# Residual parts of five tiles moved from VectorE to ScalarE and GpSimd, and the first tiles of the K/V loop reordered

## The chip, the cores and the metric

The kernel runs on one core of one Trainium2 chip. The metric is the device time of one execution in microseconds (us). The engines are called by their short names: PE (TensorE), DVE (VectorE), ACT (ScalarE), POOL (GpSimd) and SP (SyncE, which here issues DMAs).

## What is computed

One transformer-like block on x of 2 x 1024 tokens with 512 features, all in float32. Six modulation vectors (sa, ca, ga, sb, cb, gb) per batch come from `silu(c) @ wmod`. Cut to what matters:

```python
h = layernorm(x) * (1 + ca) + sa
Xn = layernorm(h) * gamma + beta
Q, K, V = split(Xn @ W_in + b_in)
K, V = rotary(K), rotary(V)                       # the first 256 of 512 features are turned
A = 0.5 * sum_tokens(K/|K| * V/|V|) + 0.5          # one row of 512 per batch
x2 = x + ga * ((A * Q) @ W_out + b_out + h)
h2 = layernorm(x2) * (1 + cb) + sb
out = x2 + gb * (shared_expert(h2) + top-2 of 8 routed experts(h2))
```

## The kernel before

The 2048 tokens are 16 tiles of 128 tokens (`t`, NT = 16; NB = 8 tiles per batch). Every matrix product of full accuracy is done as three products of a high and a low part (`product3`, lines 1819 to 1821: hi*hi, hi*lo, lo*hi), so each operand needs a high part, written by ACT with a rounding copy, and a low part, which DVE forms as the difference (`weights_hi`/`weights_lo`, `tokens_hi`/`tokens_lo`). Every engine has its own instruction stream, written by hand in program order; semaphores join them, and an instruction that waits holds up all that stands behind it on its engine.

**The K/V loop (about 20 to 152 us).** For each tile: DVE `x_statistics(t)` takes mean and variance of x (lines 1121 to 1123), POOL `first_power(t)` raises the variance to the power -1/2 (L593), DVE `modulated(t)` forms h (L1137, L1140) and its statistics (L1157 to L1160), POOL `second_power(t)` makes the second normalisation's factors (L598, L599), ACT `normed(t)` applies them (L735), PE `transposes(t)` turns the tile (L1867), ACT `tokens_hi` and DVE `tokens_lo` split it (L743, L1164), PE `kv_matmul(t, 0)` and `kv_matmul(t, 1)` form K and V. ACT `k_row` copies K out of PSUM, DVE `products(t)` multiplies V and K (L1189, L1190) and turns the product with the rotary tables `cs` (L1202), ACT `k_square` and `v_square` take the norms, POOL `token_weight` makes the weight of each token, and PE `weighted_sums(t)` adds the tile into A (L1949). Bank use is double buffered by t % 2.

Between these PE carries small one-off products, the list `MISC`: the rotary tables `sin_a`, `cos_a` (tiles 0 to 3) and `sin_b`, `cos_b` (tiles 4 to 7), the rows `s1`, `c1` of batch 1, the four transposes `q0` to `q3` of W_in's Q part, and others. `SLOT_A[t]` stand between K and V of tile t, `SLOT_B[t]` behind V of tile t; all but `cos_a` use one bank, so each waits until the one before it in the list was read. ACT or DVE (`BY_VECTOR`) read them one iteration later.

**The second row loop (about 169 to 280 us).** For each tile: PE `y_matmul(t)` (A-scaled Q and W_out folded into one matrix `mw`), DVE `second_rows(t)` adds the residual part `u_of(t)` (L1355) and takes statistics, POOL `third_power(t)` (L610), DVE `ffn_rows(t)` makes h2 (L1367, L1369), PE `transposes2`, ACT `tokens2_hi` (L879, L880), DVE `tokens2_lo` (L1374). The residual part, `(1 + ca) * ga` plus a column, times the normalised x of the ring `xring`, is one DVE instruction (`residual_part`, L1343) one tile ahead; ACT `x_normed` (L867) fills the ring. `shared_in_lo(t)` (t < 4, L1106) and, at t = 6, `m_block_late` and `m_block_lo_late` (L1307, L1312) also stand on DVE; the shared expert's first chunks come into PE's stream behind tiles 6, 7, 10 and 13 (`Y_CHUNKS`), and chunk 1 waits for DVE's `s_mul_of(0, 0)` (L1382) of chunk 0. `y_matmul(t)` waits for `second_rows(t - 2)`; chunk 0 of the shared expert waits for `tokens2_lo(3)`.

Behind that stand the rest of the shared expert and the routed experts, which the diff does not touch.

## Time and profile before

| | us |
|---|---|
| median of 3 runs (lowest, highest) | 663.05 (662.36, 664.44) |
| the profiled execution: its time, its span | 664.68, 662.9 |
| busy: PE, DVE, ACT, POOL | 641.3, 495.2, 268.6, 164.7 |

The profile is one execution, followed by engine. A row of a timeline gives the start in us from the span's start, the duration in us, the engine, the source line, the operation with its tiles (written tile first), the shapes and a count, and in brackets how long the engine was idle before it and what released it. Durations of neighbouring DVE and ACT rows overlap by some hundredths, so lengths of steps are best taken from start to start. A row of the waits says who waited for whom, the total, the number of times and the longest.

### The profile page before, as it was taken

To read this page: it belongs to the slowest core of one execution; us is meant where nothing else is said; L and a number is where in the kernel's file an instruction comes from. 1 tells how busy PE (TensorE), PEld (TensorE's weight loads), DVE (VectorE), ACT (ScalarE), POOL (GpSimd) and SP (SyncE) were. 2 spreads that over 40 slices of the span, in tenths; PEclk is the share of its full clock that TensorE was granted. 3 is DMA by queue.
4 is the path that set the end of the run, shared out by engine and by line. 5 is a ranking of instruction groups with operands and counts; after the bars stand their busy time and mean duration, and the time that the engine had idled before them with its cause. 6 is when DMAs were issued, how large, how long until landed. Compare 5 with 4: busy or idle time off the path is not lost.

```text
span 662.9 us, 10578 instructions
## 1 busy us (share of the span) xinstructions
PE 641.3 (97%) x3666; PEld 531.6 (80%) x3666; DVE 495.2 (75%) x1087; ACT 268.6 (41%) x525; POOL 164.7 (25%) x211
## 2 busy tenths in 40 slices
PE   7899999999998999999999999999999999999995
PEld 3577677777876788788888888899989899899994
DVE  3987779848899788637895685569769697886953
ACT  2555354443544333511202302435537455474531
POOL 1233233320011111100000002313554445453123
PEclk9999999999999899999999999999999999999998
DMA  8913031106234262513042043446877668676145
GB/s 327 386 67 112 25 105 33 32 17 207 79 112 142 80 215 96 175 46 114 0 118 97 1 143 95 135 137 205 163 147 200 95 194 153 157 184 108 47 63 63
DMA packets 41151, 80.80 MB, mean 122 GB/s; under 512 B 5019, under 2 KB 13229, under 8 KB 40566
## 3 DMA queue, kind: packets, MB, share of 16 engines
q1 hardware_dynamic: 33382, 62.06, 28.3%
q0 software_dynamic: 7728, 18.22, 15.0%
q8 instruction: 23, 0.38, 0.2%
q14 instruction: 18, 0.15, 0.1%
HBM read 58.88 MB, written 22.56 MB: 123 GB/s over the span
## 4 chain that ended last, share of the span: by engine, by line
PE 83%; DVE 11%; issue 2%; ACT 1%; DMA 1%; POOL 1%; SPq 0%; POOLq 0%; DVEq 0%
PE bank L1819 22%; PE bank L1821 22%; PE bank L1820 22%; PE bank L2131 5%; PE bank L2106 2%; PE bank L1949 1%; PE bank L2136 1%; PE bank L1885 1%; DMA xring<-in_L_attn_X 1%; PE bank L1867 1%; PE bank L2194 1%; PE bank L2086 1%; DVE st L1121 1%; POOL out_rows L679 1%; DVE hx L1367 1%
## 5 line engine op out<-in xcount | busy, mean ns | idle before, releaser
L1819 PE MATMUL bank<-xt,sgu 128*128 128x512 f32 x176 | 70.0, 398 | 5.2 <-DVE ewst L1382 2.0
L1819 PE MATMUL bank<-ht,ew 128*128 128x256 f32 (+1 forms) x256 | 74.3, 290 | 0.0
L1820 PE MATMUL bank<-ht,ew 128*128 128x256 f32 (+1 forms) x256 | 73.1, 285 | 0.0
L1821 PE MATMUL bank<-ht,ew 128*128 128x256 f32 (+1 forms) x256 | 73.0, 285 | 0.0
L679 POOL DMA_INDIRECT out_rows<-y,si x35 | 54.8, 1565 | 73.5 <-DVE y L1748 64.0
L1821 PE MATMUL bank<-xt,sgu 128*128 128x512 f32 x176 | 69.4, 394 | 0.0
L1820 PE MATMUL bank<-xt,sgu 128*128 128x512 f32 x176 | 69.2, 393 | 0.0
L1819 PE MATMUL bank<-wkv,xt 128*128 128x512 f32 x128 | 53.8, 421 | 1.4 <-DVE xt L1164 1.4
L1820 PE MATMUL bank<-wkv,xt 128*128 128x512 f32 x128 | 50.5, 395 | 0.0
L1821 PE MATMUL bank<-wkv,xt 128*128 128x512 f32 x128 | 50.5, 394 | 0.0
L1820 PEld LDWEIGHTS bank<-ht,ew 128*128 128x128 f32 x256 | 48.2, 188 | 0.0
L1819 PEld LDWEIGHTS bank<-ht,ew 128*128 128x128 f32 x256 | 48.2, 188 | 0.0
L1821 PEld LDWEIGHTS bank<-ht,ew 128*128 128x128 f32 x256 | 48.2, 188 | 0.0
L659 POOL COPY gi<-gidx 128x5 int32 (+1 forms) x8 | 4.7, 584 | 168.8 <-DVEq L1657 130.6
L667 POOL DMA_INDIRECT picked<-h_d,gi x36 | 41.3, 1147 | 17.5 <-issue 8.5
L1819 PEld LDWEIGHTS bank<-xt,sgu 128*128 128x128 f32 x176 | 33.5, 190 | 12.5 <-DVE ewst L1382 2.3
L610 POOL TENSOR_TENSOR rs<-ve,nhalf 128x1 f32<-128x1 f32 x16 | 14.9, 933 | 98.5 <-DVE ve L1123 98.5
L1821 PEld LDWEIGHTS bank<-xt,sgu 128*128 128x128 f32 x176 | 33.4, 190 | 7.2
L1820 PEld LDWEIGHTS bank<-xt,sgu 128*128 128x128 f32 x176 | 33.5, 190 | 6.4
L1819 PE MATMUL bank<-ew,gtR 128*128 128x512 f32 (+1 forms) x96 | 38.4, 400 | 0.0
L1820 PE MATMUL bank<-ew,gtR 128*128 128x512 f32 (+1 forms) x96 | 37.9, 395 | 0.0
L1821 PE MATMUL bank<-ew,gtR 128*128 128x512 f32 (+1 forms) x96 | 37.8, 394 | 0.0
(377 smaller groups left out, 1632.8 us busy)
## 6 DMA issues: line engine op xcount, KB each, us to landing
xring<-in_L_attn_X SPq DMA_DIRECT2D x32, 256.0 KB, 2.7
ewst<-in_L_ffn_w_gate SPq DMA_DIRECT2D x8, 704.0 KB, 5.4
ewst<-in_L_ffn_w_up SPq DMA_DIRECT2D x8, 704.0 KB, 4.9
slots<-in_L_wmod SPq DMA_DIRECT2D x4, 1024.0 KB, 6.7
x_d<-rows SPq DMA_DIRECT2D x16, 256.0 KB, 2.0
h_d<-hx SPq DMA_DIRECT2D x16, 256.0 KB, 2.0
xrow<-x_d SPq DMA_DIRECT2D x16, 256.0 KB, 2.7
out_rows<-xrow SPq DMA_DIRECT2D x16, 256.0 KB, 2.0
```

The source lines that it names most:

```text
L610: pool.tensor_tensor(rs[:, 2, t:t + 1], ve[:, 2, t:t + 1], nhalf[:, 0:1], ALU.pow).then_inc(rs3_ready, 1)
L667: pool.indirect_dma_start(out=picked[par][:, j, :], out_offset=None, in_=h2_d, in_offset=bass.IndirectOffsetOnAxis(ap=gi[:, par, j:j + 1], ...
L679: pool.indirect_dma_start(out=out, out_offset=bass.IndirectOffsetOnAxis(ap=si[0:CR[j], par, j:j + 1], axis=0), in_=y[0:CR[j], j, :], in_of ...
L1121: link(dve.bn_stats(st6[:, :], row))
L1367: link(dve.scalar_tensor_tensor(hx_of(t), rows_of(t), mv2[:, t, 0:1], bc_cb[:, b, :], ALU.subtract, ALU.mult))
L1819: nc.tensor.matmul(dst, a[0], b[0], start=first, stop=False)
L1820: nc.tensor.matmul(dst, a[0], b[1], start=False, stop=False)
L1821: return nc.tensor.matmul(dst, a[1], b[0], start=False, stop=last)
L1867: last = nc.tensor.transpose(bank[T_BANKS[t % 2]][:, k * P:(k + 1) * P], hz[:, 2 + t % 2, k * P:(k + 1) * P], ident[:, :])
L1885: nc.tensor.matmul(to, pairs4[:, :].to_broadcast([P, P]), (bk, bv)[i][:, :], start=False, stop=True)\
L2106: last = nc.tensor.transpose(bank[RT_BANKS[(par + s) % 2]][:, i * P:(i + 1) * P], picked[par][:, j, k * P:(k + 1) * P], ident[:, :])
L2131: nc.tensor.matmul(bank[to[c % 2]][0:n, 0:width], packed[:, k, i * P:i * P + n], tok[part][:, k, :], start=k == 0 and not part, stop=k == ...
```

## The change

In words: (1) residual parts of tiles 2 to 6: ACT's new `residual_factor` writes the factor (row plus column) into `u`, and POOL multiplies it in place with the ring's x, behind `third_power` of the tile before; DVE's `residual_part` is left for the other tiles. (2) At t = 6 DVE runs `m_block_lo_late` behind `s_mul_of(0, 0)`. (3) PE computes V's bias row before K of tile 0, in the place of three filler matmuls. (4) DVE runs `modulated(1)` ahead of `weights_lo(0)`, and `tokens_lo(0)` behind its first chunk; ACT runs `normed(1)` two weight chunks earlier; `x_statistics(2)`, `modulated(2)` and the product of the tables come later. (5) The tables and most of `MISC` move one tile later; `products` is split, and tile 0's turning (`turned_products`) runs at t = 2; PE turns tile 2 behind V of tile 1 and adds tile 0 at t = 2.

```diff
-SLOT_A = {1: ["s1"], 2: ["sin_b"], 3: ["q0"], 4: ["q2"], 6: ["qrow"]}
-SLOT_B = {0: ["sin_a", "cos_a"], 1: ["c1"], 2: ["cos_b"], 3: ["q1"], 4: ["q3"], 5: ["mod"], 6: ["qbias"], 9: ["a0"]}
+SHARED_OUT = range(2, 7)
+SLOT_A = {2: ["s1"], 3: ["sin_b"], 4: ["q0"], 5: ["q2"], 6: ["qrow"], 7: ["q3"]}
+SLOT_B = {1: ["sin_a", "cos_a"], 2: ["c1"], 3: ["cos_b"], 4: ["q1"], 5: ["mod"], 6: ["qbias"], 9: ["a0"]}
...
             for t in range(NT):
                 third_power(t)
+                if t + 1 in SHARED_OUT:
+                    pool.wait_ge(xh_ready, t + 2)
+                    pool.tensor_tensor(u_of(t + 1), u_of(t + 1), xring[:, (NT + t + 1) % GT, :], ALU.mult)\
+                        .then_inc(x_read, 1)
...
-            weights_hi(1, (1, 2, 3))
+            weights_hi(1, (1,))
             normed(1)
+            weights_hi(1, (2, 3))
             bias_row_hi(1)
             tokens_hi(1)
-            act.wait_ge(sincos, 1)
-            nc.scalar.activation(sin, sin, ACT.Square).then_inc(sinsq, 1)
             for t in range(NT):
                 if t:
                     for name in SLOT_B.get(t - 1, ()):
                         if name not in BY_VECTOR:
                             read_misc(name)
+                    if t == 1:
+                        tokens_hi(2)
+                        k_row(1)
                     v_square(t - 1)
...
                 if t + 2 < NT:
                     normed(t + 2)
+                if t == 0:
+                    act.wait_ge(sincos, 1)
+                    nc.scalar.activation(sin, sin, ACT.Square).then_inc(sinsq, 1)
...
+            def residual_factor(t):
+
+                act.wait_ge(x2_ready, t - 1)
+                nc.scalar.activation(u_of(t), bc_g[:, t // NB, :], ACT.Identity, bias=std1[:, t:t + 1])\
+                    .then_inc(xh_ready, 1)
...
                 if t >= 2:
                     tokens2_hi(t - 2)
+                if t + 1 in SHARED_OUT:
+                    residual_factor(t + 1)
                 if t + 2 < NT:
                     x_normed(t + 2)
...
-            weights_lo(0)
-            x_statistics(2)
+            modulated(1)
+            weights_lo(0, (0,))
             tokens_lo(0)
-            modulated(1)
+            weights_lo(0, (1, 2, 3))
             bias_rows(0)
             weights_lo(1)
             bias_rows(1)
             tokens_lo(1)
+            x_statistics(2)
+            modulated(2)
             dve.wait_ge(table_in, 32)
             dve.tensor_tensor(cos, cos, sin, ALU.mult).then_inc(sincos, 1)
             for t in range(NT):
+                if t == 2:
+                    turned_products(0)
                 if t:
                     products(t - 1)
+                    if t > 1:
+                        turned_products(t - 1)
...
-                if t + 2 < NT:
+                if t == 1:
+                    tokens_lo(2)
+                if 0 < t < NT - 2:
                     modulated(t + 2)
-                if 1 <= t < NT - 1:
+                if 1 < t < NT - 1:
                     tokens_lo(t + 1)
...
-                if t and t + 1 < NT:
+                if t and t + 1 < NT and t + 1 not in SHARED_OUT:
                     residual_part(t + 1)
...
-                if t == NB - 2:
-                    for i in range(DC):
-                        m_block_lo_late(i)
                 if t < DC:
                     shared_in_lo(t)
                 if t in Y_CHUNKS:
                     s_mul_of(0, Y_CHUNKS[t])
+                if t == NB - 2:
+                    for i in range(DC):
+                        m_block_lo_late(i)
...
             transposes(0)
-            keep_busy(3)
+            bias_row(1)
             for t in range(NT):
                 kv_matmul(t, 0)
-                if t == 0:
-                    bias_row(1)
-                if t + 1 < NT:
+                if t + 1 < NT and t != 1:
                     transposes(t + 1)
+                if t == 2:
+                    weighted_sums(0)
                 for name in SLOT_A.get(t, ()):
                     misc(name)
                 kv_matmul(t, 1)
+                if t == 1:
+                    transposes(2)
                 for name in SLOT_B.get(t, ()):
                     misc(name)
-                if t:
+                if t >= 2:
                     weighted_sums(t - 1)
```

## Rows read from the trace of the kernel before

**Rows 1.** Waits of PE from 60 to 280 us: line, releaser, total, times, longest.

```profile
PE bank L1819 <- DVE rows L1355: 2.3, 2, 1.2
PE bank L1819 <- DVE ewst L1382: 2.0, 1, 2.0
PE bank L1819 <- DVE xt L1374: 2.0, 1, 2.0
```

**Rows 2.** Timeline of PE, 0 to 62 us.

```profile
19.06 0.66 PE L1867 MATMUL bank<-ident,hz 128*128 128x128 f32 x4 [1.01 <-ACT hz L735]
...
25.49 1.06 PE L1856 MATMUL bank<-slots,gb_col 128*32 128x512 f32 x8
...
27.45 0.66 PE L1867 MATMUL bank<-ident,hz 128*128 128x128 f32 x4
...
32.29 0.48 PE L1819 MATMUL bank<-wkv,xt 128*128 128x512 f32 x1
...
41.12 0.41 PE L1949 MATMUL bank<-prod,wtok 128*32 128x256 f32 x2
...
58.02 0.50 PE L1819 MATMUL bank<-wkv,xt 128*128 128x512 f32 x1
```

**Rows 3.** Timeline of DVE, 0 to 62 us.

```profile
17.36 2.74 DVE L1170 SCALAR_TENSOR_TENSOR wkv<-slots,gb_col,wkv 128x512 fp32r<-128x512 f32 x4
...
29.46 1.21 DVE L1276 TENSOR_TENSOR slots<-slots 128x1024 f32<-128x1024 f32 x1
...
36.83 0.75 DVE L1137 SCALAR_TENSOR_TENSOR hz<-xring,mv,bc_c 128x512 f32<-128x512 f32 x1
...
39.48 0.68 DVE L1164 TENSOR_TENSOR xt<-bank,xt 128x512 fp32r<-128x512 f32 x1
40.07 0.69 DVE L1121 BATCH_NORM_STATS2 st<-xring 128x6 f32<-128x512 f32 x1
```

**Rows 4.** Timeline of ACT, 0 to 62 us.

```profile
30.70 1.06 ACT L818 ACTIVATE slots<-slots 128x1024 f32<-128x1024 f32 x1 [1.96 <-DVE slots L1276]
...
40.49 0.81 ACT L735 ACTIVATE hz<-hz,nm,rs 128x512 f32<-128x512 f32 x1 [1.75 <-POOL nm L599]
```

**Rows 5.** Timeline of POOL, 0 to 62 us.

```profile
1.22 0.28 POOL L583 TENSOR_SCALAR_AFFINE_SELECT ident<-ident 128x128 f32<-128x128 f32 x1 [0.24 <-POOL ident L582]
1.47 0.20 POOL L585 MEMSET gw<- 128x128 f32 x1
1.61 0.12 POOL L586 MEMSET ones<- 128x32 f32 x1
...
40.26 0.19 POOL L599 TENSOR_TENSOR nm<-mv,rs 128x1 f32<-128x1 f32 x1
```

**Rows 6.** Timeline of POOL, 152 to 240 us.

```profile
174.96 0.55 POOL L610 TENSOR_TENSOR rs<-ve,nhalf 128x1 f32<-128x1 f32 x1 [20.36 <-DVE ve L1123]
...
193.74 0.99 POOL L610 TENSOR_TENSOR rs<-ve,nhalf 128x1 f32<-128x1 f32 x1 [6.29 <-DVE ve L1123]
```

**Rows 7.** Timeline of DVE, 152 to 240 us.

```profile
188.20 0.69 DVE L1374 TENSOR_TENSOR xt<-bank,xt 128x512 fp32r<-128x512 f32 x1 [1.15 <-ACT xt L880]
...
193.57 0.74 DVE L1343 SCALAR_TENSOR_TENSOR u<-bc_c,std,xring 128x512 f32<-128x512 f32 x1
...
194.84 0.74 DVE L1367 SCALAR_TENSOR_TENSOR hx<-rows,mv,bc_gb 128x512 f32<-128x512 f32 x1
...
213.72 1.29 DVE L1312 TENSOR_TENSOR mw<-xrow,mw 128x512 fp32r<-128x512 f32 x2
...
216.13 0.68 DVE L1382 TENSOR_TENSOR ewst<-ewst,bank 128x512 f32<-128x512 f32 x1
```

**Rows 8.** Timeline of ACT, 152 to 240 us.

```profile
188.05 0.82 ACT L867 ACTIVATE xring<-xring,nm,rs 128x512 f32<-128x512 f32 x1
```

**Rows 9.** Stretches of 2 us: busy time of each engine, then PE's granted clock (full is 1.00).

```profile
218.00:220.00 2.00, 2.00 (x7) 1.53 (x6) 1.93 (x6) 0.00 (x0) 0.99 (x1) 0.50 0.36 131
220.00:222.00 2.00, 2.00 (x8) 1.61 (x7) 1.88 (x3) 0.00 (x0) 0.00 (x0) 0.65 0.41 131
```

More of the change, by code:

```diff
@@ L64 @@
 M_BLOCKS = 2 * DC - 1
+SHARED_OUT = range(2, 7)
 Y_CHUNKS = {6: 0, 7: 1, 10: 2, 13: 3}
-MISC = ["sin_a", "cos_a", "s1", "c1", "sin_b", "cos_b", "q0", "q1", "q2", "q3", "mod", "qrow", "qbias", "a0", "a1"]
+MISC = ["sin_a", "cos_a", "s1", "c1", "sin_b", "cos_b", "q0", "q1", "q2", "mod", "qrow", "qbias", "q3", "a0", "a1"]
 BY_VECTOR = ("c1", "mod", "qbias", "a0", "a1")
-SLOT_A = {1: ["s1"], 2: ["sin_b"], 3: ["q0"], 4: ["q2"], 6: ["qrow"]}
-SLOT_B = {0: ["sin_a", "cos_a"], 1: ["c1"], 2: ["cos_b"], 3: ["q1"], 4: ["q3"], 5: ["mod"], 6: ["qbias"], 9: ["a0"]}
+SLOT_A = {2: ["s1"], 3: ["sin_b"], 4: ["q0"], 5: ["q2"], 6: ["qrow"], 7: ["q3"]}
+SLOT_B = {1: ["sin_a", "cos_a"], 2: ["c1"], 3: ["cos_b"], 4: ["q1"], 5: ["mod"], 6: ["qbias"], 9: ["a0"]}
 def build(nc, X, W_in, b_in, W_out, b_out, gamma, beta, gate_w, w_gate, w_up, w_down,
@@ L793, in scaled_q @@
                 elif k == 0:
-                    act.wait_ge(misc_mm, MISC.index("qbias") + 1)
+                    act.wait_ge(misc_mm, MISC.index("q3") + 1)
                     act.wait_ge(wo_lo, DC)
@@ L826, in _ @@
                     a_rows(0)
-                k_row(t)
-                if 1 <= t < NT - 1:
+                if t != 1:
+                    k_row(t)
+                if 1 < t < NT - 1:
                     tokens_hi(t + 1)
@@ L866, in x_normed @@
                 act.wait_ge(x_in[n % GT], 16 * (n // GT + 1))
-                nc.scalar.activation(xring[:, n % GT, :], xring[:, n % GT, :], ACT.Identity, bias=nm1[:, t:t + 1],
-                                     scale=rs[:, 0, t:t + 1]).then_inc(xh_ready, 1)
+                last = nc.scalar.activation(xring[:, n % GT, :], xring[:, n % GT, :], ACT.Identity, bias=nm1[:, t:t + 1],
+                                            scale=rs[:, 0, t:t + 1])
+                if t not in SHARED_OUT:
+                    last.then_inc(xh_ready, 1)
+            def residual_factor(t):
+                act.wait_ge(x2_ready, t - 1)
+                nc.scalar.activation(u_of(t), bc_g[:, t // NB, :], ACT.Identity, bias=std1[:, t:t + 1])\
+                    .then_inc(xh_ready, 1)
             def tokens2_hi(t):
@@ L1191, in products, with turned_products @@
                                   pairs(ksb[:, t % 2, 0:ROT]), ALU.mult).then_inc(multiplied, 1)
+            def turned_products(t):
                 dve.wait_ge(multiplied, t + 1)
@@ L1282, in _ @@
                             read_misc(name)
-                if t + 2 < NT:
+                if t == 1:
+                    tokens_lo(2)
+                if 0 < t < NT - 2:
                     modulated(t + 2)
-                if 1 <= t < NT - 1:
+                if 1 < t < NT - 1:
                     tokens_lo(t + 1)
@@ L1294, in _ @@
             products(NT - 1)
+            turned_products(NT - 1)
             def m_block(b, i):
```

## The prediction

> **What bounds the kernel now.** I read the busy table first: PE is busy in 97% of the span, so a change can win at most where PE waits or idles. The forty slices put those places at the start, near 200 us and at the end. Then PE's own waits. Between 60 and 280 us there are four waits on DVE, 6.3 us in all, and all lie in the second row loop [rows 1]: two on L1355 (`second_rows`), one on L1374 (`tokens2_lo`, ahead of the shared expert's chunk 0) and one on L1382 (`s_mul_of`, ahead of chunk 1). DVE's timeline shows why: in the tiles t = 2 to 6 it runs without a gap [rows 7], while ACT and POOL stand idle for most of each tile. The granted clock is the third view: after the last of these waits PE ran at 0.50 of full speed from 218 us, and 0.65 in the next 2 us [rows 9]. [...] At the start, PE computes the bias row of V (25.49 to 27.45, 1.96 us) only behind K of tile 0, though it ran fillers just before K [rows 2]. From 41.12 us, where tile 0 is added, it is packed to 58.02, where K of tile 4 starts [rows 2].
>
> **The change at the start of the loop.** Times here are on the axis of the rows of before.
>
> Bias row: PE finishes turning tile 0 at about 19.5 and computes V's bias row to 21.5, in the fillers' place. DVE: `modulated(1)` takes 39.48 - 36.83 = 2.65 us [rows 3], from 17.36 to 20.0. Then one chunk of `weights_lo` (2.74 / 4, some 0.67 from start to start), `tokens_lo(0)` (0.6) to 21.3, three chunks to 23.3, `bias_rows(0)` to 23.9. So PE starts K at 21.5 and never waits for a chunk; V follows to 28.1, and K of tile 1 starts at 28.15 instead of 32.29 [rows 2]. Of these 4.1 us, 0.85 are only the four tables' transposes put off, so 3.3 us are won here.
>
> What is late next is the work that was moved behind. DVE is done with `tokens_lo(1)` at 27.85. `x_statistics(2)` takes 1.0 (its first row is at 40.07 [rows 3]), POOL's power 0.55 and hand-overs 0.1, so `modulated(2)` starts at 29.6 and its last operation ends at 32.3. Behind it on DVE stands the product of the tables, two inputs from SBUF, 1.21 us [rows 3]. POOL's power for `second_power(2)` is then asked for 0.1 us after that product has begun. A POOL power takes 0.55 us alone and 0.99 us when a DVE operation with two SBUF inputs is running as it starts: the one at 193.74 ended 0.4 us behind the DVE operation of 193.57 [rows 6, 7]. So POOL ends at 34.0, its product (0.19 [rows 5]) at 34.2, ACT's `normed(2)` (0.81 [rows 4]) at 35.05. PE has finished K and V of tile 1 at 34.3: **first stall, 0.8**. ACT then squares the table (1.06 [rows 4]) to 36.0, which PE's `cos_a` waits for (0.15), and only then `tokens_hi(2)` (0.6), DVE `tokens_lo(2)` (0.68): K of tile 2 starts at 37.25 where PE is free at 36.5: **second, 0.75**. `modulated(3)` begins as `tokens_lo(2)` ends, and from its start to the end of `normed` pass (40.49 + 0.81) - 36.83 = 4.47 us [rows 3, 4]; K takes 3.05. **Third, 1.4**: PE turns tile 3 at 41.65. Behind `normed(3)` ACT reads `sin_a` and `cos_a` (1.2), DVE turns the products of tile 0 (0.7), and PE, which now has `weighted_sums(0)` ahead of V of tile 2, gets it at 43.45 instead of 41.12: **fourth, 1.4**.
>
> From there PE has the same work as before from 41.12 to 58.02 (16.9 us), plus `s1` and `c1` (0.95 each, done earlier before), less K and the turning of tile 2 (3.55, done by now), less `q0` and `q1` (0.95, still to come): 14.3, so K of tile 4 starts at 57.75, with 0.95 of `q0` and `q1` owed. 58.7 against 58.02: the start is **0.7 us slower**. The 3.3 us won are given back in four waits. If the product of the tables did not hold POOL up, all of it would come 0.9 earlier (-0.2).
>
> The other `MISC` slots are later by a tile, each behind a read that is in time: PE's slack to `tokens_lo` at tile 3 is over 1 us by the same sums. SP waits for `cos_b` with `load_mod(3)` and four loads of x behind it; both are wanted only at tiles 5 and 8, so I cost this at nothing; a late load would hold `x_statistics(8)`.
>
> **The change in the second row loop.** DVE loses five instructions of 0.67 us from start to start (193.57, L1343 [rows 7]). ACT gains five of some 0.6 us, in a stream that waits for PE anyway; `x_normed` behind it (188.05, 0.82 [rows 8]) is wanted a tile later. POOL gains five products of 128 x 512 with two SBUF inputs. Their duration M is not in the trace. A 128 x 1 product is 0.19. A memset, one output stream, takes 0.12 at 32 columns and 0.20 at 128, 0.85 ns a column [rows 5]; 0.19 + 0.43 = 0.62 is the lower bound. The operation with one input and one output took 0.28 for 128 columns [rows 5], 1.5 ns a column, 0.75 a stream; with three streams 0.19 + 1.16 = 1.35, the upper bound. I take M = 1.0, between the two-stream figure (0.95) and that.
>
> Two things decide what this is worth. First, part of the 0.67 hid POOL's power: `ffn_rows(3)` could start no earlier than the power, which alone would end 0.51 before 194.84 [rows 6, 7]. So a tile gains 0.51. Second, the product on POOL starts as the power ends, which is as DVE starts `ffn_rows`, two operations with two SBUF inputs. The rows show that POOL makes no progress while such a DVE operation runs. They do not show the reverse; a resource that is exclusive one way I take as exclusive the other way, so DVE stands still for M once a tile. And if DVE came first each time, `second_rows(t + 1)` would wait for the product instead. The bounds are 0 and M a tile; I take M.
>
> [...]
>
> The sum, by tile: t = 1 gains nothing, since DVE waits at t = 2 for PE's turning anyway (188.20, 1.15 idle [rows 7]). At t = 2 the product starts as ACT's factor lands (188.05 + 0.65), just before `ffn_rows(2)`, which was at 188.20 + 0.60: +M - 0.1 [rows 7, 8]. At t = 3, 4 and 5: +M - 0.51 each. At t = 6 `s_mul_of(0, 0)` no longer stands behind `m_block_lo_late` (216.13 - 213.72 = 2.41 [rows 7]). Chunk 1 starts later by 4M - 1.63 - 2.41 = 4M - 4.04. With M = 1.0 that is **0.0**; 0.62 gives -1.6, 1.35 gives +1.4. `y_matmul(8)` needs the low parts of `m` a whole chunk later. Behind chunk 1 PE is bound by itself, so the shift stays.
>
> The fall of the clock: it followed a 2.0 us wait. With these sums that wait shrinks to about 0.8 while the one ahead of `y_matmul(6)` grows to some 2.6; at the start PE is idle for 2.8 of the 3.1 us ahead of `weighted_sums(0)`. I count one fall, as before, somewhere.
>
> **Total**: 0.7 + 0.0 = +0.7. The profiled execution took 664.68, so it would be 665.4; the median of before is 1.6 lower, so 663.05 + 0.7 = **663.7**, no change that a measurement of this kernel can tell (0.3%, 2 us).
>
> **The rivals.** *(A) DVE is not held up by POOL*, 0.28. Then t = 3, 4, 5 gain 0.51 each, chunk 0 starts 1.02 + 0.66 = 1.7 earlier, chunk 1 is freed by DVE 1.53 + 2.41 = 3.9 earlier, and PE can take 2.0 + 1.7 = 3.7 of it [rows 1]. The clock does not fall there: -1.7. With the start's +0.7: -4.7, 658.3. For it speaks that no row shows DVE waiting for POOL; against it that POOL so plainly waits for DVE. *(B) Slower by the clock*, 0.18. The two stalls around tile 3 bring PE's clock down at the start, where PE alone sets the end from then on, and the later fall stays as well: 0.7 + 1.7 = +2.4, and with M at its upper bound +3.8; 665.5 to 666.9. It decides from two falls instead of one. For it: one wait of 2.0 was enough in [rows 9]. Against: each of these stalls is shorter than that one. *(C) The four waits at the start do not come*, since the chains are shorter than I add them: the 3.3 us stay, and 663.05 - 3.3 = 659.8, 0.08. PE did not wait there before, which speaks for short chains; but then tile 2 was formed before K of tile 1. *(D) Forecast*, 0.46: 662.0 to 665.0.
>
> **Chances.** Faster by over 0.3% is A and most of C: 0.35. Within: 0.47. Slower: B: 0.18. The range of 8 in 10 reaches from A, 658.0, to the lower part of B, 666.0.
>
> **What would show it.** In the profile after: K of tile 1 at 28.2; PE idle before the turnings of tiles 2 and 3, before K of tile 2 and before `weighted_sums(0)`, released by ACT and DVE; POOL's power for tile 2 at 1.5 us beside the tables' product. In the second loop: POOL products of about 1 us, and L1367 or L1369 longer or later by as much; L1355 of tile 4 at +1.4; chunk 1 at the old place behind chunk 0. If L1367 follows POOL's power at once and L1369 follows 0.78 later while POOL multiplies, A is right. The prediction fails if M lies outside its bounds, or if DVE and POOL share without waiting.

## The result and the profile after

| | before | after |
|---|---|---|
| median of 20 runs each (lowest, highest), us | 663.64 (662.23, 665.63) | 664.92 (663.23, 666.62) |
| the profiled execution: time, span, us | 664.68, 662.9 | 663.63, 661.9 |
| busy PE, DVE, ACT, POOL, us | 641.3, 495.2, 268.6, 164.7 | 639.8, 496.9, 271.9, 170.7 |

The ratio is 1.0021, with an interval of 1.0011 to 1.0031: the changed kernel takes 1.3 us longer (0.7 to 2.1), within the 0.3% that I called no change. The forecast was +0.7. The profiled executions stand the other way round, 1.0 us shorter after, so their rows must be read for causes and not for the total. The largest reason is the clock: before had its fall at 218 us inside the span [rows 9], and after has full clock there. Columns are as in [rows 9].

```profile
218.00:220.00 2.00, 2.00 (x11) 1.65 (x10) 1.97 (x4) 0.38 (x1) 0.00 (x0) 1.00 0.00 0
220.00:222.00 2.00, 2.00 (x11) 1.65 (x10) 1.93 (x5) 0.00 (x0) 0.94 (x1) 1.00 0.67 183
```

**The start.** PE's timeline after, 16 to 62 us, answers [rows 2]. Its axis lies 0.69 us earlier: the first turning of a tile is at 18.37 and was at 19.06, because PE waited less for the first loads (0.3 us ahead of 19 us, where it was 1.1); in every other trace below this row lies between 18.1 and 18.5 too, whatever start the kernel has. Differences below are taken from it.

```profile
18.37 0.66 PE L1900 MATMUL bank<-ident,hz 128*128 128x128 f32 x4 [1.01 <-ACT hz L740]
18.96 1.06 PE L1889 MATMUL bank<-slots,gb_col 128*32 128x512 f32 x8
...
27.52 0.39 PE L1852 MATMUL bank<-wkv,xt 128*128 128x512 f32 x1
...
34.33 0.66 PE L1900 MATMUL bank<-ident,hz 128*128 128x128 f32 x4 [0.58 <-ACT hz L740]
...
36.58 0.47 PE L1852 MATMUL bank<-wkv,xt 128*128 128x512 f32 x1 [0.58 <-DVE xt L1185]
...
40.87 0.66 PE L1900 MATMUL bank<-ident,hz 128*128 128x128 f32 x4 [1.03 <-ACT hz L740]
...
42.73 0.41 PE L1982 MATMUL bank<-prod,wtok 128*32 128x256 f32 x2 [1.20 <-DVE tq L1226]
...
56.92 0.50 PE L1852 MATMUL bank<-wkv,xt 128*128 128x512 f32 x1
```

The bias row of V stands ahead of K of tile 0 (18.96), K of tile 1 starts at 27.52, and then come the four waits, 0.58, 0.58, 1.03 and 1.20, released by ACT, DVE, ACT and DVE. K of tile 4 starts at 56.92, 57.61 on the axis of before. POOL's row for the first wait shows the power of tile 2 at 1.46 us, and DVE's row the product of the tables that it ran beside:

```profile
31.70 1.46 POOL L599 TENSOR_TENSOR rs<-ve,nhalf 128x1 f32<-128x1 f32 x1 [2.85 <-DVE mv L1181]
```

```profile
31.54 1.21 DVE L1302 TENSOR_TENSOR slots<-slots 128x1024 f32<-128x1024 f32 x1
```

**The second row loop.** First POOL, then DVE, 178 to 218 us. L611 is the power, L641 the new product; L1400 and L1402 are the two instructions of `ffn_rows` (L1367 and L1369 before), L1415 is `s_mul_of`.

```profile
188.76 1.83 POOL L641 TENSOR_TENSOR u<-u,xring 128x512 f32<-128x512 f32 x1 [1.25 <-ACT u L886]
...
194.55 0.55 POOL L611 TENSOR_TENSOR rs<-ve,nhalf 128x1 f32<-128x1 f32 x1 [3.96 <-DVE ve L1144]
195.07 1.31 POOL L641 TENSOR_TENSOR u<-u,xring 128x512 f32<-128x512 f32 x1
```

```profile
188.72 0.74 DVE L1400 SCALAR_TENSOR_TENSOR hx<-rows,mv,bc_gb 128x512 f32<-128x512 f32 x1
189.49 1.66 DVE L1402 SCALAR_TENSOR_TENSOR hx<-hx,rs,bc_s 128x512 f32<-128x512 f32 x1
...
195.14 1.78 DVE L1400 SCALAR_TENSOR_TENSOR hx<-rows,mv,bc_gb 128x512 f32<-128x512 f32 x1
...
216.11 0.68 DVE L1415 TENSOR_TENSOR ewst<-ewst,bank 128x512 f32<-128x512 f32 x1
```

The first instruction of `ffn_rows` took 0.74 in [rows 7] (L1367) and takes 1.78 where it starts 0.07 behind POOL's product: DVE stands still for 1.04. At tile 2 L1400 started first and ran in 0.74; the product began 0.04 behind it and lasted 1.83 instead of 1.3, so here POOL was held up, and then L1402 was held up for 0.91. PE's waits from 62 to 280 us answer [rows 1]:

```profile
PE bank L1852 <- DVE rows L1388: 2.7, 2, 1.5
PE bank L1852 <- DVE xt L1407: 1.7, 1, 1.7
PE bank L2229 <- DVE hx L1402: 0.9, 1, 0.9
PE bank L1852 <- DVE ewst L1415: 0.8, 1, 0.8
```

The sum is 6.1 us where it was 6.3. The wait ahead of chunk 1 shrank from 2.0 to 0.8, and a new one of 0.9 and a longer one of 1.5 stand ahead of it. PE starts chunk 1 at 216.84 after and 216.87 before, which is 47.86 and 47.80 us behind its first row of `y_matmul(0)`: in the second loop the change moves chunk 1 by 0.06.

### The profile page after: what moved, and what is told of

Same layout as the page of the kernel before. It is cut to its first block, busy times and chain, and to the rows that moved or that the text cites. A ratio compares the mean times of both kernels' runs of the same rounds, so it can differ in the third digit from the quotient of the medians.

```text
span 661.9 us, 10571 instructions
## 1 busy us (share of the span) xinstructions
PE 639.8 (97%) x3660; PEld 529.8 (80%) x3660; DVE 496.9 (75%) x1082; ACT 271.9 (41%) x530; POOL 170.7 (26%) x216
## 4 chain that ended last, share of the span: by engine, by line
PE 82%; DVE 10%; DMA 2%; issue 2%; ACT 1%; POOL 1%; SPq 1%; POOLq 0%; DVEq 0%
PE bank L1852 22%; PE bank L1854 21%; PE bank L1853 21%; PE bank L2166 5%; PE bank L2141 2%; PE bank L1982 1%; PE bank L2171 1%; DVE hx L1400 1%; PE bank L1918 1%; DMA xring<-in_L_attn_X 1%; DVE wkv L1191 1%; DMA out_rows<-xrow 1%; PE bank L1900 1%; PE bank L2229 1%; PE bank L2121 1%
## 5 line engine op out<-in xcount | busy, mean ns | idle before, releaser
L1852 PEld LDWEIGHTS bank<-ht,ew 128*128 128x128 f32 x256 | 48.2, 188 | 0.0
L1854 PEld LDWEIGHTS bank<-ht,ew 128*128 128x128 f32 x256 | 48.2, 188 | 0.0
L611 POOL TENSOR_TENSOR rs<-ve,nhalf 128x1 f32<-128x1 f32 x16 | 12.8, 798 | 91.0 <-DVE ve L1144 91.0
```

The lines of the kernel that those rows point to most:

```text
L611: pool.tensor_tensor(rs[:, 2, t:t + 1], ve[:, 2, t:t + 1], nhalf[:, 0:1], ALU.pow).then_inc(rs3_ready, 1)
L1852: nc.tensor.matmul(dst, a[0], b[0], start=first, stop=False)
L1854: return nc.tensor.matmul(dst, a[1], b[0], start=False, stop=last)
```

## The experiments

My theory after the first profile: the start loses some 0.6 us in four waits; in the second loop DVE's standstill of 1 us a tile eats what was taken off DVE, and moving `m_block_lo_late` pays for the rest. The rivals: the residual parts bring nothing or the start does all the damage, the clock makes the difference, or the standstill comes from something else than POOL's reading. Every time below is a median with the lowest, the highest and the number of runs; ratios are to the kernel before, timed on the same chip.

### The start alone

The three edits of the first loop are kept (bias row, tile 1 ahead of the low parts, tables a tile later); the second loop is that of before.

```diff
-SHARED_OUT = range(2, 7)
...
-                if t + 1 in SHARED_OUT:
-                    residual_factor(t + 1)
```

> Only the start of the K/V loop is reordered (parts 3 to 5), the second row loop is that of before. Theory of the prediction: the bias row and the earlier first tile win 3.3 us, four waits of PE in tiles 1 to 3 give them back; K of tile 4 comes 0.5 to 0.7 us later with the same work done, so the time is that of before +0.5 to +0.7 us. Rival: the start wins its 3.3 us in the end and the whole cost lies in the second row loop; then this kernel is 2 to 3 us faster than before.

665.48 (663.88 to 667.25, 12), ratio 1.0024 (1.0011 to 1.0037): 1.6 us slower by the ratio (0.7 to 2.5), 1.3 by the medians. The start is the whole of the loss. PE's waits at the start are those of after. The 0.5 or 0.6 that the rows of the start show is at the lower end of that interval; what may be missing is taken up below.

### The second loop alone, and its two halves

The second loop of the change with the start of before (both halves), then only the move of `m_block_lo_late`, then only the sharing of the residual parts.

```diff
-                if t == NB - 2:
-                    for i in range(DC):
-                        m_block_lo_late(i)
                 if t < DC:
                     shared_in_lo(t)
                 if t in Y_CHUNKS:
                     s_mul_of(0, Y_CHUNKS[t])
+                if t == NB - 2:
+                    for i in range(DC):
+                        m_block_lo_late(i)
```

> Only parts 1 and 2: the residual parts of tiles 2 to 6 on ACT and POOL, and the low parts of m behind the first s_mul. The start is that of before. Theory: DVE stands still for about 1 us per tile, which gives back what the five removed instructions and the moved low parts win; chunk 1 of the shared expert starts where it did before: 0.0 us, or down to -1.7 us where the PE clock no longer falls behind chunk 1. Rival (the start alone is at fault): 3 us or more faster than before.

663.87 (662.76 to 666.51, 12), ratio 0.9997 (0.9984 to 1.0011): no difference.

> Only part 2: the low parts of m behind the first s_mul. Theory: the wait of PE ahead of chunk 1 was 2.0 us and DVE frees it 2.4 us earlier, so it goes altogether: -2.0 us, and with the fall of the clock that followed it gone as well down to -3.7 us. Rival: y_matmul(8) or second_rows(7) then comes late and the gain is given back: 0.

662.01 (660.82 to 663.0, 12), ratio 0.9967 (0.9955 to 0.9978): 2.2 us faster. The wait ahead of chunk 1 is gone from PE's list, 62 to 280 us:

```profile
PE bank L1819 <- DVE rows L1355: 2.3, 2, 1.2
PE bank L1819 <- DVE xt L1374: 2.0, 1, 2.0
```

> Only part 1: the residual parts of tiles 2 to 6 on ACT and POOL; the low parts of m stand where they stood. Theory: with the standstill of about 1 us a tile (one tile 0.9, three tiles 1.0 - 0.5 each), chunk 1 starts some 2.4 us later than before: +2.4 us. Rival, without the standstill: DVE is 1.5 us ahead at tile 6, -1.5 us.

667.51 (665.94 to 668.65, 6), ratio 1.0048 (1.0029 to 1.0067): 3.2 us slower. The same list:

```profile
PE bank L1834 <- DVE ewst L1397: 3.2, 1, 3.2
PE bank L1834 <- DVE rows L1370: 2.7, 2, 1.5
PE bank L1834 <- DVE xt L1389: 1.7, 1, 1.7
PE bank L2209 <- DVE hx L1384: 0.9, 1, 0.9
```

The wait ahead of chunk 1 is 3.2 here and 0.8 in after, apart by 2.4: the length of `m_block_lo_late` that the forecast took from [rows 7]. Chunk 1 starts 50.26 us behind `y_matmul(0)`, 2.46 later than before, where +2.4 was expected. The rest of the 3.2 goes with the clock: this trace has two falls, the one of [rows 9] and another at 20 to 26 us, and five of the six executions have the lower mean clock that goes with two (see the part on the clock). So the move gains 2.2 by itself, the sharing loses 3.2 by itself and 2.0 on top of the move, and the two together are nothing. The residual parts, as the change shares them, are a loss.

### What in POOL's product holds DVE up

Both kernels below are the changed one with another operation at L641. Both leave part of the computation out, so that the routing behind it differs and their totals say nothing (717.84 and 718.6 us); only rows of the second loop are read. First a memset in place of the product, which leaves out the residual parts of tiles 2 to 6 and reads nothing:

```diff
-                    pool.tensor_tensor(u_of(t + 1), u_of(t + 1), xring[:, (NT + t + 1) % GT, :], ALU.mult)\
+                    pool.memset(u_of(t + 1), 0.5)\
```

> The changed kernel with POOL's five products replaced by a fill of the same 128x512 tile, which reads nothing (the residual parts of tiles 2 to 6 are therefore not computed). All waits and semaphores stay. Theory (DVE stands still because POOL is reading SBUF): the first or second operation of ffn_rows takes 0.75 us in all five tiles instead of 1.7 to 1.8, and chunk 1 of the shared expert starts 3 us or more earlier against y_matmul(0). Rival (it is POOL's write to the tile, or the tile's address, that holds DVE up): those operations stay at 1.2 us or more.

```profile
182.23 0.53 POOL L641 MEMSET u<- 128x512 f32 x1
```

```profile
182.32 0.75 DVE L1400 SCALAR_TENSOR_TENSOR hx<-rows,mv,bc_gb 128x512 f32<-128x512 f32 x1 [0.67 <-POOL rs L611]
```

The DVE instruction that starts 0.09 behind the memset takes 0.75: it isn't held up, and neither L1400 nor L1402 is at any of the five tiles (0.74 or 0.75). Chunk 1 starts 43.89 us behind `y_matmul(0)`, 4.0 earlier than in after. Then one input instead of two, which leaves x out of the residual parts:

```diff
-                    pool.tensor_tensor(u_of(t + 1), u_of(t + 1), xring[:, (NT + t + 1) % GT, :], ALU.mult)\
+                    pool.tensor_scalar(u_of(t + 1), u_of(t + 1), 0.5, None, ALU.mult)\
```

> The changed kernel with POOL's five products of two tiles replaced by a product of one tile with a constant, in place (the x of tiles 2 to 6 is left out of the residual part). Theory: DVE stands still for as long as POOL reads; with one input instead of two the operation is shorter, so ffn_rows' stretched operation takes some 1.3 to 1.5 us instead of 1.77. [...]

```profile
190.43 2.04 POOL L641 TENSOR_SCALAR u<-u 128x512 f32<-128x512 f32 x1 [1.91 <-ACT u L886]
...
196.09 1.49 POOL L641 TENSOR_SCALAR u<-u 128x512 f32<-128x512 f32 x1
```

```profile
190.37 0.74 DVE L1400 SCALAR_TENSOR_TENSOR hx<-rows,mv,bc_gb 128x512 f32<-128x512 f32 x1
191.15 0.98 DVE L1402 SCALAR_TENSOR_TENSOR hx<-hx,rs,bc_s 128x512 f32<-128x512 f32 x1
...
196.14 1.10 DVE L1400 SCALAR_TENSOR_TENSOR hx<-rows,mv,bc_gb 128x512 f32<-128x512 f32 x1
```

I expected a shorter operation on POOL and 1.3 to 1.5 us for L1400. L1400 takes 1.10, a standstill of 1.10 - 0.74 = 0.36, and POOL's instruction is not shorter but longer than the two-input product (1.49 against 1.29). So the standstill is 0, 0.36 and 1.03 for no, one and two inputs, beside lengths on POOL of 0.53, 1.49 and 1.29. It takes a read on POOL's side: the memset writes the same tile and holds nothing up.

Whether the standstill follows the length of POOL's operation is not shown. No row has the one-input operation without a two-input DVE instruction beside it, and POOL can be held up as well: at tile 2, where L1400 came first, the same operation lasts 2.04. The 1.49 may therefore hold the 0.74 us of L1400; an estimate of the operation's own length is then 1.49 - 0.74 = 0.75. What makes two inputs cost nearly three times one is open too.

The hold-up shows in both directions: DVE behind POOL here, POOL behind DVE in the power of 1.46 beside the tables' product and in the 1.83 and 2.04 of tile 2. DVE's standstill isn't the whole of what is left of POOL's operation: L1400 at 195.14, held up for 1.04, gets on 0.20 us before the product's end at 196.38. For one input it is 0.36 of 1.49 us, less than the whole, even if the operation's own length is only the 0.75 of the estimate.

### The product beneath DVE's statistics

If reading beside a two-input DVE instruction is what costs (1.03 us for the product, 0 for the memset), then the product should stand where DVE runs instructions with one input. Between `second_rows` and the power there are three: L1142 to L1144 in after, 1.0 us in all. So the product is released with the rows of a tile and put ahead of its power, and ACT's factor ahead of `tokens2_hi`; the start is that of before, and `m_block_lo_late` is moved.

```diff
             for t in range(NT):
-                third_power(t)
                 if t + 1 in SHARED_OUT:
                     pool.wait_ge(xh_ready, t + 2)
+                    pool.wait_ge(x2_ready, t + 1)
                     pool.tensor_tensor(u_of(t + 1), u_of(t + 1), xring[:, (NT + t + 1) % GT, :], ALU.mult)\
                         .then_inc(x_read, 1)
+                third_power(t)
...
+                if t + 1 in SHARED_OUT:
+                    residual_factor(t + 1)
                 if t >= 2:
                     tokens2_hi(t - 2)
-                if t + 1 in SHARED_OUT:
-                    residual_factor(t + 1)
```

> Start as before; second row loop as changed, but POOL makes the product of tile t+1 ahead of third_power(t), as soon as second_rows(t) has written its row, while DVE runs the statistics (one SBUF input), and ACT forms the factor ahead of tokens2_hi. Theory: product (1.2 to 1.3 us) and statistics (1.1 us) overlap without holding each other up, third_power starts at most 0.3 us later; ffn_rows' operations take 0.75 us; chunk 1 starts 3 us or more earlier than before, and the time is 3 to 5 us below before. Rival (POOL's power comes late by the whole product and ffn_rows waits for it): no gain over the kernel with parts 1 and 2 alone, within 1 us of before.

659.26 (659.06 to 660.29, 6), ratio 0.9942 (0.9929 to 0.9956): 4.1 us below 663.4 for the kernel before, 3.8 by the ratio (2.9 to 4.7). POOL, then DVE:

```profile
192.07 1.29 POOL L641 TENSOR_TENSOR u<-u,xring 128x512 f32<-128x512 f32 x1 [5.74 <-DVE rows L1371]
193.31 0.55 POOL L611 TENSOR_TENSOR rs<-ve,nhalf 128x1 f32<-128x1 f32 x1
```

```profile
191.18 0.74 DVE L1371 SCALAR_TENSOR_TENSOR rows<-u,mv,bank 128x512 f32<-128x512 f32 x1
191.96 0.69 DVE L1137 BATCH_NORM_STATS2 st<-rows 128x6 f32<-128x512 f32 x1
192.69 0.18 DVE L1138 BATCH_NORM_AGGREGATE mv<-st 128x2 f32<-128x6 f32 x1
...
192.98 0.68 DVE L1390 TENSOR_TENSOR xt<-bank,xt 128x512 fp32r<-128x512 f32 x1
193.90 0.76 DVE L1383 SCALAR_TENSOR_TENSOR hx<-rows,mv,bc_gb 128x512 f32<-128x512 f32 x1 [0.24 <-POOL rs L611]
```

The product runs in 1.29 beside the statistics, which keep their 0.69, and beside L1390, whose one input is a bank of PSUM, at 0.68. `ffn_rows` waits 0.24 for the power and runs in 0.76. The same five products on POOL that cost 1 us each are now nearly free. PE's waits, 62 to 300 us:

```profile
PE bank L1835 <- DVE rows L1371: 2.0, 2, 1.1
PE bank L1835 <- DVE xt L1390: 0.6, 1, 0.6
PE bank L2223 <- ACT srow L861: 0.4, 1, 0.4
```

Three us are left of 6.3, and chunk 1 starts 44.42 us behind `y_matmul(0)`, 3.4 earlier than before. The rest of the gain goes with the clock: the trace has no fall ahead of its last microseconds, and by the mean clock (see the part on the clock) neither have five of the six executions, where 14 of the 17 of before beside them have one. The next run shares the residual parts of all tiles from 2 on:

```diff
-SHARED_OUT = range(2, 7)
+SHARED_OUT = range(2, NT)
```

> The kernel with the early product (4.1 us below before) with the residual parts of all tiles from 2 on given to ACT and GpSimd, not only tiles 2 to 6. If DVE still bounds the loop behind tile 6: up to 1.2 us more, 4.1 to 5.3 below before. Rival, PE alone bounds the loop there: no gain, 4.1 below before within 0.5.

659.43 (658.64 to 660.23, 6), ratio 0.993 (0.9915 to 0.9944), 4.1 us below before: no gain that can be told from the version with five tiles. The forecast had PE alone set the end behind chunk 1. That isn't quite so: from chunk 1 to PE's matmul behind the last wait of the loop it is 48.0 us in after and in the version with five tiles, with one wait on `second_rows` of 1.15 us in it, and 48.2 here with a wait of 1.36. Taking residual parts off DVE doesn't shorten that wait, so the shift of chunk 1 stays, as forecast.

### Mending the start

The first attempt: the tables' product one place earlier (ahead of `modulated(2)`), ACT's square ahead of `normed(2)`, and the reads of `sin_a` and `cos_a` ahead of `normed(3)`; second loop of before.

```diff
+            dve.wait_ge(table_in, 32)
+            dve.tensor_tensor(cos, cos, sin, ALU.mult).then_inc(sincos, 1)
             modulated(2)
-            dve.wait_ge(table_in, 32)
-            dve.tensor_tensor(cos, cos, sin, ALU.mult).then_inc(sincos, 1)
...
+                if t == 1:
+                    for name in SLOT_B[1]:
+                        read_misc(name)
                 if t + 2 < NT:
                     normed(t + 2)
```

> Start reordered as in the change, with two orders put right: DVE forms the product of the tables ahead of modulated(2), between x_statistics(2) and it, and ACT squares the table ahead of normed(2) and reads sin_a and cos_a ahead of normed(3). Second row loop as before. Theory of the four waits: the first shrinks from 0.6 to about 0.1 (POOL's power is no longer held up by the tables' product), the second goes down by some 0.3 more, the fourth (1.2 us, for the turned products of tile 0) goes; third (1.0) stays. That is 2.1 us less than with the changed start, so 0.8 us below before. Rival (the waits are not what the start costs): the time stays at 1.3 us above before.

663.3 (662.27 to 666.27, 12), ratio 0.9997 (0.9987 to 1.0007): 0.2 below before (0.9 below to 0.5 above), where 0.8 below was expected; that the waits aren't what the start costs (1.3 above) is refuted. The fourth wait is gone and the first stayed, since another power of POOL now ran beside the tables' product:

```profile
28.19 1.46 POOL L593 TENSOR_TENSOR rs<-ve,nhalf 128x1 f32<-128x1 f32 x1 [7.56 <-DVE ve L1132]
```

Second attempt, in the changed kernel with the early product: the tables' product behind `x_statistics(3)` instead, the reads ahead of `normed(3)` as above.

```diff
-            dve.wait_ge(table_in, 32)
-            dve.tensor_tensor(cos, cos, sin, ALU.mult).then_inc(sincos, 1)
...
                 if t + 3 < NT:
                     x_statistics(t + 3)
+                if t == 0:
+                    dve.wait_ge(table_in, 32)
+                    dve.tensor_tensor(cos, cos, sin, ALU.mult).then_inc(sincos, 1)
```

> The changed kernel with two things moved. In the second row loop GpSimd's product stands ahead of the power, beneath DVE's statistics, which took 4.1 us off the kernel before when done alone. At the start the product of the tables stands behind x_statistics(3), after POOL's powers for tiles 1 and 2, and sin_a and cos_a are read ahead of normed(3). My theory, that the changed start loses its gain in the four waits and that the tables' product is the cause of the first and the ACT queue of the fourth: POOL's second power takes 0.55, the first wait and the fourth are gone or under 0.3 us, the start is even with the kernel before or 0.5 better, and the time is 4 to 5 us below before. Rival, that the hold-up only moves again, as it did when the product was put one place earlier: another POOL power at 1.0 to 1.5 us, the waits in another place with the same sum, and 2.5 to 3.5 us below before.

659.28 (658.33 to 660.48, 6), ratio 0.9934 (0.9918 to 0.9949): 4.3 us below 663.56. POOL, from 31 us, and PE's waits of the start:

```profile
31.50 0.55 POOL L599 TENSOR_TENSOR rs<-ve,nhalf 128x1 f32<-128x1 f32 x1 [2.85 <-DVE mv L1185]
...
32.50 1.46 POOL L594 TENSOR_TENSOR rs<-ve,nhalf 128x1 f32<-128x1 f32 x1 [0.19 <-DVE ve L1148]
```

```profile
PE bank L1905 <- ACT hz L741: 2.1, 2, 1.0
PE bank L1857 <- DVE xt L1189: 0.6, 1, 0.6
PE bank L1941 <- ACT slots L849: 0.4, 1, 0.4
```

The power for the first wait is 0.55 and that wait is gone, as is the fourth; the 2.1 for ACT are the wait ahead of the first turning (1.0, in before too) and the third. The product now holds up the next power (1.46 at 32.50), and PE has a new wait of 0.4 for the squared table. Theory and rival are both half right: the second and third waits stay. The kernel is not measurably faster than the one with the early product and the start of before (ratios 0.9934 and 0.9942, intervals overlapping). The best versions lie 4.1 to 4.3 us below before, and so some 5.5 below the changed kernel.

The last two runs take the start apart. The bias row of V ahead of K, in the kernel before and alone:

```diff
             transposes(0)
-            keep_busy(3)
+            bias_row(1)
             for t in range(NT):
                 kv_matmul(t, 0)
-                if t == 0:
-                    bias_row(1)
```

> The kernel before with the bias row of V ahead of K of tile 0 and nothing else of the changed start. My theory: the 3.3 us come from having V's bias row done early AND tile 1 formed early; with the old order of DVE and ACT, K of tile 1 (its low parts of the tokens) is not ready sooner, and the gap that the fillers filled only moves: within 0.5 us of before. Rival, the early bias row is worth its own 2.0 us by itself and the rest of the changed start is what loses: 1.5 to 2 us below before.

663.33 (662.07 to 664.86, 12), ratio 0.9994 (0.9983 to 1.0006): nothing that can be told from before. PE has the bias row done and then waits for tile 1, which ACT and DVE form no sooner:

```profile
25.65 0.66 PE L1867 MATMUL bank<-ident,hz 128*128 128x128 f32 x4 [1.06 <-ACT hz L735]
```

And the changed kernel with the early product and its own start:

> The changed kernel with the early product and ACT's factor ahead of tokens2_hi, its own start kept. If the start's loss (1.3 to 1.6 us alone) and the early product's gain (4.1 alone) add up: 2.5 to 2.8 us below before, 3.8 to 4.1 below the changed kernel. Rival, they share a bound, so that one hides the other: 1.5 or less below before.

661.54 (661.08 to 662.09, 6), ratio 0.9964 (0.995 to 0.9978): 2.0 below the median of before, 2.4 by the ratio. Sum of the parts: 1.6 - 4.1 = -2.5, or -2.2 with the 3.8 of the ratio. The start's loss and the second loop's gain add up, so each part can be judged by itself.

### Where the rest of the start's loss is

From the first turning of a tile to `weighted_sums(2)`, PE took 57.47 - 19.06 = 38.41 us before and, in the kernel with the start alone, 56.35 - 18.36 = 37.99 with `q0` and `q1` (0.95) still owed: +0.53. To the matmul behind the first wait of the second loop it is 198.62 - 19.06 = 179.56 and 198.51 - 18.36 = 180.15: +0.59. The runs say +1.6. The rows of DVE in the kernel with the start alone show a place that the forecast doesn't have, some 140 us later:

```profile
340.77 0.68 DVE L1507 TENSOR_TENSOR srow<-bank,bc_gb 128x512 f32<-128x512 f32 x1
342.99 0.69 DVE L1509 TENSOR_TENSOR xrow<-xrow,srow 128x512 f32<-128x512 f32 x1 [1.53 <-DMA xrow<-x_d]
```

and PE, behind the one-hots that DVE forms next:

```profile
344.63 0.38 PE L2085 MATMUL bank<-hot_col,hot_row 128*128 128x240 f32 x1 [0.35 <-DVE hot_col L1468]
```

PE waits three times there, 0.35 to 0.51. Before, the same DVE row is at 341.56 with no idle time ahead of it, and PE has one wait of 0.41. The read of x is issued at 338.43 here and at 338.53 before, so it is not issued later, it lands later. From the end of the last wait of [rows 1] to PE's matmul with `gtS` behind these rows it is 374.22 - 266.47 = 107.75 us before and 375.67 - 266.40 = 109.27 here, 1.5 more; 108.18 in after, 0.4 more.

The traces divide without exception. In all eight with V's bias row early, the two that leave work out among them, DVE waits for this read (0.45 to 1.55 us); in the six with the start of before it doesn't. Leaving out the two, the stretch is 0.4 to 1.5 us longer in the first group, a fall of the clock taken off in one of them, and that of before to 0.1 us in the five other variants of the second. The size, though, can't be taken from the start alone: its trace and that of the first mending, the two with 1.5 us, are of the slowest of their twelve executions (667.25 and 666.27, 1.8 and 3.0 above their medians). The four others have waits of 0.45 to 0.48, which make the stretch 0.4 to 0.5 longer. With that the start comes to 0.6 + 0.4 = 1.0, inside the measured 0.7 to 2.5. The same sum for V's bias row alone is 178.93 - 179.56 = -0.63 up to the second loop and +0.46 behind it, so -0.2, and measured are -0.4 (-1.1 to 0.4). It is one execution for each kernel, and no run here changes the read alone: that the new start is the cause is argued, and why the read lands later is open.

## Why the prediction was right, point by point

**The total**, +0.7 forecast and +1.3 (0.7 to 2.1) measured, holds, and so does its split in kind. Start: forecast +0.7, measured +1.6 (0.7 to 2.5). Second loop: 0.0, measured -0.2 (-1.1 to 0.7). The 663.7 was added to a median of before of 663.05, from three executions; with twenty it is 663.64, which makes up half of the distance to 664.92. That the number holds is in part luck: the start lacks a term, the length of POOL's product was too short where the standstill was right, and the falls of the clock became fewer, which the sum doesn't have.

**The four waits** came at the four places, with the releasers named. Sizes, forecast and measured: 0.8 and 0.58; 0.15 + 0.75 and 0.58; 1.4 and 1.03; 1.4 and 1.20. Each is 0.2 to 0.4 shorter than I added it; which of the hand-overs in each sum is too long I did not take apart. K of tile 1 was forecast at 28.15 and is at 28.21 on the axis of before; K of tile 4 at 57.75 and is at 57.61. POOL's power was forecast at some 1.5 beside the tables' product and took 1.46. Rival C, that the waits would not come, is refuted. The statement that all of it would be 0.9 earlier if POOL were not held up doesn't hold either: with the power at 0.55 (second attempt) the first wait went, but K of tile 2 came only 0.4 earlier than in after and the third wait stayed at 1.04, so a single hold-up did not carry the whole chain.

**What the start's sum lacked** is a term for what lies behind the start. I took PE's work from 41 us on as the same, and it is so up to the second loop (+0.53 and +0.59). The wait at 344 us, for a read that no row of before waits for, wasn't in the sum; by the traces it is mostly 0.4 to 0.5 us, 1.5 in the slowest executions. It is the one place found that would put the measured loss above the +0.6 of the start's rows; its cause is not shown.

**POOL's product M.** Bounds 0.62 to 1.35, taken 1.0: it lasts 1.29 to 1.31 and holds DVE up for 1.03, so the term of the sum, DVE's standstill, was right to 0.03. The step that said the two are the same was wrong by 0.26: DVE starts 0.07 behind the product and gets on 0.20 before its end. That it did no harm is luck. The 1.0 was chosen between two scalings of other operations, the real length lies near the upper bound, and with 1.3 for M the sum 4M - 4.04 would have been +1.2. At tile 2 the forecast had the product start first; it started 0.04 behind L1400, and L1402 paid 0.91 where 0.9 was forecast. Taking the exclusion as mutual, which no row of before showed, was right: rival A, no hold-up at all, is refuted by L1400 at 1.78, where it took 0.74 in [rows 7]. Its price was of the right size: A gave the second loop -5.4 (its -4.7 less the start's +0.7), 3.7 of it in PE's waits and 1.7 for the clock. With the hold-up taken away by placing, the time is 4.1 below before: 3.4 by the start of chunk 1, and the rest by fewer falls.

**m_block_lo_late** was priced at 2.41 and PE's wait differs by 2.4 between the two kernels that differ in it. The loss of the sharing alone, 4 x 1.0 - 1.63 = +2.4 forecast, was +3.2 (1.9 to 4.4), of which chunk 1 shows 2.46.

**The chunks.** `y_matmul(6)` was to wait some 2.6: there are 0.9 and 1.5 ahead of it. Chunk 1 was to keep its wait of about 0.8: 0.8. Chunk 1 starts 0.07 later than the shift of the start (+0.59) makes it; 0.0 was forecast.

**The clock.** I counted one fall somewhere. The profiled execution of after has none ahead of its last microseconds. In the kernel with the changed start and the early product it fell where rival B put it, behind the waits around tile 3:

```profile
42.00:44.00 2.00, 1.36 (x10) 0.46 (x11) 1.97 (x4) 0.37 (x1) 0.00 (x0) 0.87 0.00 0
44.00:46.00 2.00, 2.00 (x5) 1.29 (x4) 1.93 (x4) 2.00 (x7) 1.27 (x2) 0.50 0.00 0
46.00:48.00 2.00, 2.00 (x8) 1.56 (x8) 1.93 (x6) 0.55 (x2) 0.73 (x2) 0.78 0.00 0
```

That costs 0.26 + 1.0 + 0.44 = 1.7 us, the price that the forecast gave a fall in A and B; it comes from [rows 9], as 2 x 0.5 + 2 x 0.35. Taken over stretches of 1 us, the same sum gives 1.7 for each of the thirteen falls ahead of the last microseconds, and in no trace is a stretch below 0.50. In time, a fall near 21 us cost less: with only `m_block_lo_late` moved, the trace has one there, and from the first turning to the matmul behind the first wait of the second loop PE takes 180.57 us against 179.56 before, 1.0 more.

How often the clock falls can be read from the mean granted clock, which is on record for single executions. The fourteen traces give the scale: 0.997 or 0.998 in the three without a fall ahead of the last microseconds, 0.994 to 0.996 in the nine with one, 0.991 and 0.992 in the two with two. By this scale, with 0.993 taken as one and 0.989 as two, 10 of the 20 executions of after have no fall (median 664.1), nine have one (666.0) and one has two. Of the 63 executions of before timed beside the experiments 10 have none (median 662.8), 52 have one, and one has two. So the changed kernel has fewer falls, and they hide a part of its loss: between the executions without a fall it is 1.3 us, though these ran on different chips.

Where the clock fell in the traces goes with the wait ahead of chunk 1. All five with a wait of 2.0 us or more there (before, the start alone, its first mending, V's bias row alone, the sharing alone) have a fall between 216 and 224 us; none of the nine with 0.8 or less has. The four waits of the start are less certain: of the five kernels that have them all, three have a fall near 44 us (the one above and the two that leave work out), after and the start alone have none there. So a fall where rival B put it comes in some executions; that the waits bring it about is not shown. But B added this fall to the later one, and two falls come in one of the 20 executions.

## What to carry to other kernels

Work given to an idle GpSimd had a price on VectorE here when it read SBUF while VectorE ran an instruction with two SBUF inputs: 1.03 us for each two-input product of 128 x 512, 0.36 for a one-input operation, 0 for a memset. Before moving work there, write down what VectorE runs in the stretch where it will fall. Beneath statistics (0.69), an aggregate (0.18) and an instruction whose second input is in PSUM (0.68) the product took its 1.29 us and lengthened none of them; that was the place for it. Here the same five products cost 2.0 us in one place (ratios 0.9997 against 0.9967, both with `m_block_lo_late` moved) and saved some 1.7 in another (0.9942 against 0.9967, and PE's chunk 1 1.1 earlier). And time each part of a combined change by itself: this one held a gain of 2.2 us, a loss of 2.0 that another place turns into a gain, and a loss of 1.6, and looked like no change.

## What the runs showed of the hardware

- A two-input VectorE instruction held up by GpSimd (128 x 512, float32): 1.03 us by a two-input product of 1.29 us, 0.36 by a one-input operation of 1.49 us, 0 by a memset of 0.53 us. VectorE's statistics, and an instruction with one of its inputs in PSUM, ran at their usual length beside the two-input product, and it at 1.29.
- GpSimd's power on 128 x 1 elements took 0.55 us alone, 0.99 behind a two-input VectorE instruction of 0.74 and 1.46 behind one of 1.21, at 31.70 us in after, at 28.19 in the first mending and at 32.50 in the second.
- The hold-up went both ways: started 0.04 and 0.06 us behind a two-input VectorE instruction, the two-input product lasted 1.83 instead of 1.29 and the one-input operation 2.04 instead of 1.49. The one-input operation was never seen without such an instruction beside it, so its own length is open.
- TensorE's granted clock went from 1.00 to 0.50 of full for some 3 us at different places: between 216 and 224 us in all five traces with a wait of 2.0 us or more ahead of chunk 1 and in none of the nine with 0.8 or less, near 44 us in three of five with the same four waits, and near 21 us in four of the six with the start of before.
- The mean granted clock of an execution counts these falls: 0.997 or 0.998 without one, 0.994 to 0.996 with one, 0.991 or 0.992 with two, in fourteen traces.
